# Two 3x3 convolutions on TensorE: a round of sixteen 32x32 products issued row group by row group

## The reference

```python
x = x + _L0_conv_ref(_gn(x), w_real, w_imag, b_real, b_imag)  # complex 3x3 convolution of the 2-D spectrum
x = x + _L1_conv_ref(_gn(x))          # u, v = halves of the channels; each row gated by the sign of a dot product
x = x + conv2d(_gn(x), L2_conv_W)     # 3x3, padding 1
x = x + conv2d(_gn(x), L3_conv_weight.reshape(16, 16, 3, 3))   # 3x3, padding 1
```

## Time and profile before

| | |
|---|---|
| median of the runs | 4946.78 us (2 runs, 4939.90 to 4953.67) |
| profiled execution | 4956.67 us |
| its span in the trace | 4954.9 us |
| TensorE busy | 4608.3 us, 93% |
| VectorE busy | 2922.7 us, 59% |
| ScalarE busy | 2496.7 us, 50% |
| mean granted TensorE clock | 0.966 |

### The profile page before, as it was taken

How to read it: one execution, slowest core, us unless ns; L and a number is a source line. 1 busy time by engine, 2 the same in 40 slices (tenths; PEclk the granted TensorE clock), 3 DMA queues, 4 the chain that set the end, 5 groups by cost and what they waited for, 6 DMA issues and landing times.

```text
span 4954.9 us, 222809 instructions
## 1 busy us (share of the span) xinstructions
PE 4608.3 (93%) x84784; PEld 2932.1 (59%) x84784; DVE 2922.7 (59%) x10604; ACT 2496.7 (50%) x7097; POOL 3.2 (0%) x14
## 2 busy tenths in 40 slices
PE   3699999999999999999999999999999999988898
PEld 0265666556656566555665556655665566655566
DVE  0377743777347771776717775277743777357770
ACT  4355445554455645554455544555445554444435
POOL 0000000000000000000000000000000000000000
PEclk9899999999999999999999999999999999999999
DMA  5344124440244404442044421444124440332104
GB/s 165 90 126 125 43 60 138 125 123 23 88 134 122 120 4 122 132 125 85 17 138 126 124 62 42 136 125 121 42 66 135 123 125 19 92 101 70 53 3 139
DMA packets 294845, 471.79 MB, mean 95 GB/s; under 512 B 22288, under 2 KB 97104, under 8 KB 294224
## 3 DMA queue, kind: packets, MB, share of 16 engines
q1 hardware_dynamic: 294224, 462.41, 31.1%
HBM read 328.10 MB, written 134.22 MB: 93 GB/s over the span
## 4 chain that ended last, share of the span: by engine, by line
PE 90%; issue 3%; DVE 3%; DMA 2%; SPq 1%; ACT 1%; ACTq 0%; DVEq 0%
PE ps L1224 34%; PE ps L1144 19%; PE ps L1129 18%; PE ps L1137 5%; PE ps L1005 5%; PE ps L1153 4%; DMA shared<-t_strip 2%; PE ps L1249 1%; PE ps L1049 0%; SPq L388 0%; PE ps L1050 0%; PE ps L1076 0%; PE ps L1198 0%; PE ps L1276 0%; PE ps L1091 0%
## 5 line engine op out<-in xcount | busy, mean ns | idle before, releaser
L1224 PE MATMUL ps<-x,conv_s 32*32 32x512 f32 x49104 | 1723.8, 603 | 33.3 <-issue 33.0
L1224 PEld LDWEIGHTS ps<-x,conv_s 32*32 32x32 f32 x49104 | 1224.7, 104 | 500.4 <-issue 249.8
L531 ACT ACTIVATE x<-ps,vec 128x256 f32 (+1 forms) x1024 | 490.1, 494 | 1001.5 <-PE ps L1144 1001.5
L1144 PE MATMUL ps<-hil,shared 128*128 128x256 f32 x4096 | 993.9, 386 | 0.0
L1144 PEld LDWEIGHTS ps<-hil,shared 128*128 128x128 f32 x4096 | 741.8, 191 | 272.5 <-issue 194.0
L772 DVE SCALAR_TENSOR_TENSOR shared<-xin,trig 128x256 f32<-128x256 f32 x2048 | 817.2, 438 | 57.2
L599 ACT ACTIVATE shared<-ps,vec 64x512 f32<-64x512 f32 (+1 forms) x768 | 525.1, 684 | 443.5 <-PE ps L1224 433.2
L1129 PE MATMUL ps<-shared 32*32 32x512 f32 x16384 | 666.6, 613 | 0.5 <-issue 0.5
L784 DVE COPY vsb<-ps 128x512 f32<-128x512 f32 x512 | 330.0, 686 | 567.7 <-PE ps L1129 567.7
L768 DVE TENSOR_SCALAR xin<-xin,vec 128x512 f32<-128x512 f32 x512 | 247.0, 482 | 610.5 <-DMA out<-shared 368.6
L588 ACT ACTIVATE x<-ps,vec 128x512 f32 x512 | 347.3, 684 | 466.4 <-PE ps L1224 466.4
(11 more groups left out here) (164 smaller groups left out, 2662.4 us busy)
## 6 DMA issues: line engine op xcount, KB each, us to landing
shared<-x SPq DMA_DIRECT2D x512, 256.0 KB
xin<-x SPq DMA_DIRECT2D x512, 256.0 KB
out<-shared SPq DMA_DIRECT2D x512, 256.0 KB
shared<-t_strip SPq DMA_DIRECT2D x576, 96.0 KB, 3.4
hil<-t_hil SPq DMA_DIRECT2D x1, 560.0 KB, 3.4
trig<-t_trig SPq DMA_DIRECT2D x1, 512.0 KB, 4.3
x<-t_bias SPq DMA_DIRECT2D x1, 512.0 KB, 5.0
x<-w_mix SPq DMA_DIRECT2D x1, 288.0 KB, 3.2
```

The lines of the kernel that those rows point to most:

```text
L531: ins = nc.scalar.activation(split_in(strip_of(s))[:, q, :], split_in(ps[:, bank, :])[:, q, :], ACT.Identity, bias=v1(MEAN), accum_out=sum ...
L1144: mm = pe.matmul(split_in(ps[:, BY + 2 * odd + e, :])[:, int(q < 2), :], xt[:, e, q, :], hil[:, q, 0:HALF], start=False, stop=True, skip_g ...
L1224: mm = pe.matmul(ps[TM * cg:TM * cg + TM, banks[k], :], conv_s[TM * rg:TM * rg + TM, kw, second, :], x1[TM * rg:TM * rg + TM, of, kw:kw + ...
```

## The change

`taps` issues all sixteen products of a round in one call, with the row group as the outermost loop: four products of row group 0, one on each column group (two first, two second, in both layers), then those of row groups 1, 2 and 3. The products, their tiles, banks and start and stop flags are the same. Since both parts are issued by one call, both parts' waits come ahead of it, and `halved` is raised by the last first product in row group 3, which is the fourteenth of its round.

```diff
-                def taps(n, p, banks, outputs, second, kw, done=None):
-
-                    for k in range(2):
-                        for m, cg, operands in outputs(2 * p + k):
-                            if operands[second] is not None:
-                                of, rg = operands[second]
-                                only = operands[1 - second] is None
-                                mm = pe.matmul(ps[TM * cg:TM * cg + TM, banks[k], :], conv_s[TM * rg:TM * rg + TM, kw, second, :],
-                                               x1[TM * rg:TM * rg + TM, of, kw:kw + N], start=(kw == 0 and (second == 0 or only)),
-                                               stop=(second == 1 and kw == TAPS - 1), skip_group_check=True)
-                    if kw == TAPS - 1:
-                        mm.then_inc((halved, convolved)[second], 1)
+                def taps(outputs, *parts):
+
+                    for rg in range(TILES):
+                        for second, p, banks, kw in parts:
+                            for k in range(2):
+                                for m, cg, operands in outputs(2 * p + k):
+                                    if operands[second] is None or operands[second][1] != rg:
+                                        continue
+                                    of, only = operands[second][0], operands[1 - second] is None
+                                    mm = pe.matmul(ps[TM * cg:TM * cg + TM, banks[k], :], conv_s[TM * rg:TM * rg + TM, kw, second, :],
+                                                   x1[TM * rg:TM * rg + TM, of, kw:kw + N], start=(kw == 0 and (second == 0 or only)),
+                                                   stop=(second == 1 and kw == TAPS - 1), skip_group_check=True)
+                            if kw == TAPS - 1 and rg == TILES - 1:
+                                mm.then_inc((halved, convolved)[second], 1)
...
                 for slot in range(PAIRS * TAPS + LAG2):
+                    parts = ()
...
-                        taps(n, PAIRS - 1 - n, banks2(n), outputs2, 0, kw)
+                        parts += ((0, PAIRS - 1 - n, banks2(n), kw),)
                     n, kw = (slot - LAG2) // TAPS, (slot - LAG2) % TAPS
                     if n >= 0:
                         if kw == 0:
                             pe.wait_ge(halved, i * (2 * PAIRS) + n + 1)
                             due()
-                        taps(n, PAIRS - 1 - n, banks2(n), outputs2, 1, kw)
+                        parts += ((1, PAIRS - 1 - n, banks2(n), kw),)
+                    taps(outputs2, *parts)
```

More of the change, by code:

```diff
@@ L1285, in first3 @@
                         due()
-                    taps(n, n, banks3(n), outputs3, 0, kw)
+                    return 0, n, banks3(n), kw
                 def second3(n, kw):
@@ L1292, in second3 @@
                         due()
-                    taps(n, n, banks3(n), outputs3, 1, kw)
+                    return 1, n, banks3(n), kw
                 prepare_at = dict(zip(U_AT + C_AT, (prepare_u1, prepare_u2, column_parts, column_turn, column_sums)))
@@ L1299, in image @@
                         prepare_at[n](i + 1)
+                    parts = ()
                     if n < PAIRS:
-                        first3(n, kw)
+                        parts += (first3(n, kw),)
                     if slot >= LAG3:
-                        second3((slot - LAG3) // TAPS, (slot - LAG3) % TAPS)
+                        parts += (second3((slot - LAG3) // TAPS, (slot - LAG3) % TAPS),)
+                    taps(outputs3, *parts)
             with pe.Fori(0, B - 1) as i:
```

## The result

| | before | after |
|---|---|---|
| median of the runs | 4946.78 us | 4992.52 us (2 runs, 4987.44 to 4997.60) |
| ratio | | 1.0096, 95% interval 1.0064 to 1.0128 |
| span of the profiled execution | 4954.9 us | 4995.7 us |
| layer 2, first to last product, sum of 8 images | 844.0 us | 844.0 us |
| layer 3, the same | 986.8 us | 1032.8 us |

The kernel is 0.96% slower, 46 us, where 30 us were forecast. The last three rows of the table are worked out from the starts and ends of the convolution products in the trace. They say at once that the sum came out near for another reason than the one given: layer 2 gained nothing that shows in its sum, and layer 3 lost 46 us, not 80.

A forecast was written before the change was run, and what follows sets the result against it. TensorE's pace was taken to bound the kernel. Layer 2's -50 us and layer 3's +80 us made +30 us: 4987 us beside the profiled execution, 4977 us beside the median, range 4900 to 5070 us.

The forecast's parts named there:

- the 80 taken: Layer 3: the forecast's loss of 80 us, rounded from a worked sum of +82, with bounds 0 and +130 us.
- The order inside a round costs nothing: Both layers: issuing products row group by row group was taken as 0 us.
- Rival 3: Both layers: one row group's loads go one by one, 0.02 us more for twelve of sixteen; 5060 us, chance 0.12.
- rival 4: Rounds: loads wait for their row-group neighbour's product, 3.5 us more per round; about 10,300 us, chance 0.05.
- Rival 1: Rounds: loader stops of 0.29 to 0.33 us vanish; about 4897 us, chance 0.14 together with Rival 5.
- Layer 2's gain of 50 us: Layer 2: halved wait moved to the round's head, 2.79 us per pair for 3.11, until VectorE limits it: -50 us.
- So the three rounds should run like those of the mix: Layer 2: a pair costs a mix's 2.51 us of loads plus a 0.28 us pause, 0.32 us less than before.
- Rival 2: Layer 2 gains nothing, its pace being set otherwise; only layer 3's loss remains: 5027 us, chance 0.14.
- Layer 3's loss by an array that runs empty: Layer 3: halved, raised two products before its wait, empties the array once per pair: 3.51 us instead of 3.10.
- the working's +82: Layer 3: 9.9 us for each of seven images plus 13.1 us for image 8, summed to +82 us.
- Rival 5: Layer 3: halved is raised early enough, the array doesn't run empty; about 4900 us, chance 0.14 together with Rival 1.
- TensorE waits for it: Layer 3, kernel before: loader stands still 0.21 us and restarts 0.12 us after ScalarE's 2.09 us eviction ends.

The follow-up runs named there:

- e2: Kernel before, with the row group outermost inside each of the two old calls and the halved wait left mid-round: 4940.24 us, ratio 0.9992.
- e1: Changed kernel's merged call with both waits at the head, but products in the old diagonal order: 4986.56 us, ratio 1.0087 against the kernel before.
- e7: Changed kernel with the column group outermost in place of the row group: 4996.87 us, ratio 1.0107 against the kernel before.
- e5: The change in layer 2 alone, layer 3 keeping the old calls: 4938.39 us, ratio 0.9987 against the kernel before.
- e8: Changed kernel with layer 2's lag LAG2 cut from 4 to 3: 5099.17 us, ratio 1.0304 against the kernel before.
- e3: Kernel before, layer 3's stores writing one of each strip's eight rows (32 KB instead of 256 KB): 4881.70 us, ratio 0.9863.
- e6: The change in layer 3 alone, layer 2 keeping the old order: 5001.10 us, ratio 1.0109 against the kernel before.
- e4: Changed kernel with layer 3's stores writing one of each strip's eight rows: 4963.87 us, ratio 1.0032 against the kernel before.
- e9: Kernel before, layer 3's odd strip evicted by one instruction instead of two and its store split into two 128 KB DMAs: 5020.14 us, ratio 1.0149.
- e11: Changed kernel with layer 3's lag LAG3 raised from 3 to 4: 5017.73 us, ratio 1.0151 against the kernel before.

## Why the prediction was right, and where it wasn't

The direction, the size to within 16 us and the mechanism of the loss were right. Two terms were not, and their misses cancelled in part: 50 us too much gain in layer 2, 34 us too much loss in layer 3 beside the 80 taken. That the total came out within 16 us is in part luck: with the loss of layer 3 as forecast and layer 2 as it is, it would have been 50 us off.

- **The order inside a round costs nothing: right.** e2 (0.9992), e1 (the loss without a new order) and e7 (as after) show it from several sides. The loads of a full burst still take 0.27 us with four neighbours in one row group, and no piece of the four is longer than in the mix. So rivals 3 and 4 fall. (Rival 3's price was too small by its own count: 0.24 us is twelve neighbours once, and a pair has three rounds of them.) The Trainium skill's rule ("TensorE: Matmul & The Clock Gate", Part 3) that a load overlaps running products only when the row groups differ doesn't hold here: twelve of sixteen loads follow a neighbour on their own row group. The same part also lets a load into a background weight buffer go ahead; whether these loads are such, no run here tells.
- **Rival 1, the stops inside a round vanish:** it falls too. The 0.33 and 0.29 us are there in the bursts of after, e1 and e7, three orders.
- **Layer 2's gain of 50 us: wrong.** The step that failed is "So the three rounds should run like those of the mix". The mix starts on idle tiles; layer 2's tiles are still busy with the round before when the next pair begins, and its 96 loads take 2.7 to 2.9 us with a wait inside or without. e5 measures the whole of it, 0.9987. e8 shows the other half: made to start on idle tiles, layer 2 has the mix's 2.51 us and pays 1.00 us ahead of them. I took the price of a burst without the price of what lets it be one. Rival 2 (only layer 3's loss is left) is what happened, though not by growing pauses, which are 0.28 us as before. VectorE didn't hold layer 2: in the kernel after its gates are 3 to 10 us ahead of the pairs that need them. What does set 3.11 us per pair there, where rounds as close as the mix's would need 3 x 0.86 = 2.58 us, no run here settles. VectorE's traffic beside it can explain little of it: in layer 3 of image 8, where VectorE is nearly idle (0.16 us), e3 still takes 94.4 us for 31 pairs, 3.05 us each.
- **Layer 3's loss by an array that runs empty: right in mechanism and, pair by pair, in size.** 3.51 us per pair, a pause of "about 1 us" ahead of 96 loads, `evicted` covered: each stands in the rows of after. e6 puts the whole loss there, and e3 and e4 find 82 us without the full stores. That this is the working's +82 to the microsecond is chance: its addends for one of the seven images (0.49, 1.3, 0.9, 0.1, 0.1 and 6.6) give 9.5 and not 9.9 us, so its sum is 80. Rival 5 (`halved` is raised early enough) falls.
- **The size of layer 3's term: 80 taken, 46 measured.** The step is "I take 80, since TensorE also stops mid-round here for no shown reason (2.31 us in rows 10), and such a stop may fall on an empty array". The direction of that remark was right, its 2 us stood for 36. What failed under it is the 3.10 us per pair taken for the kernel before: it came from eight pairs without a stop. With the stops a pair takes 3.39 us on average in the stretches of the table (after: 3.60), and the median of all is 3.17 us. The stops were no accident of one stretch but a second limit of the kernel before, its instruction fetch, and the slower kernel meets it less.
- **"TensorE waits for it", in layer 3 of the kernel before: not supported.** A loader that starts 0.12 us after an eviction's end looked released by it. e9 shortened the evictions by 0.8 us and the intervals stayed. e11 shows what such a release looks like in a row: the idle time names ACT.

No version that writes the whole output beat the kernel before by more than the 0.13% of e5.

## What to carry to other kernels

A producer and a consumer on the same engine need other work between the raising and the waiting: here a round of sixteen products was enough, while eight left a pause of 0.90 us and two one of 1.00 us. Moving a wait from behind eight independent products to ahead of them made it the last wait, once per pair, though no work was added. A burst taken from another place of the trace has its starting state in its price: ask whether the queue was empty when it began, and what emptying it costs. And where a stop names no reason, lay the instruction queue's packets beside it: a loss elsewhere may be half paid by stops that a slower pace avoids.

## What was not expected of the hardware

- TensorE runs out of instructions beside stores: 20 stops, 45.2 us in all, in the stretches looked at before; none with stores of an eighth of the size, and 67 us less for the whole kernel.
- A strip stored as two transfers of 64 partitions each is slow: 3.85 us per pair of 512 KB, 136 GB/s, where the kernel before moves a pair in 3.1 us. It made e9 1.5% slower with less work on ScalarE, as each next image had to wait for its stores. Each half has 64 partitions in place of 128 and four rows in place of eight; which of it makes them slow wasn't tried.
